# Attention of a decoder block: where the products with the values stand in the next group, and the order of the refills

## What is computed

```python
q = (x @ Wqa @ Wqb).reshape(b, s, H, D)
kv = (x @ Wkva @ Wkvb).reshape(b, s, KVH, D, 2)
k, v = (kv[..., 0], kv[..., 1])
q = _rope(q); k = _rope(k)
scores = jnp.einsum('bqhd,bkhd->bhqk', q, k) * scale     # causal mask
w = jax.nn.softmax(scores, axis=-1)
out = jnp.einsum('bhqk,bkhd->bqhd', w, v).reshape(b, s, E)
```

## Time and profile before

| | us |
|---|---|
| median of three runs | 1338.8 |
| the profiled execution, device time | 1340.68 |
| its span | 1338.7 |
| PE, DVE, ACT, POOL busy | 1062.5, 798.1, 660.4, 423.2 |
| attention: first Exp to the last copy of sums | 194.8 to 513.8 |

### The profile page before, as it was taken

One profiled execution on the slowest core, in us unless ns is written; L12 is line 12 of the kernel. 1 busy time (PEld: TensorE's weight loads), 2 busy tenths in 40 slices (PEclk: granted clock), 3 DMA queues, 4 the chain that ended last, 5 costly groups with the idle time before them and its releaser, 6 DMA issues. The chain is left out here.

```text
span 1338.7 us, 23286 instructions
## 1 busy us (share of the span) xinstructions
PE 1062.5 (79%) x7133; PEld 781.2 (58%) x7133; DVE 798.1 (60%) x1705; ACT 660.4 (49%) x1166; POOL 423.2 (32%) x556
## 2 busy tenths in 40 slices
PE   3777058788999984884478899898989989899886
PEld 2444023343444442773367788777878777788775
DVE  4888356576777762763446646656565565654643
ACT  1334115565666674562137355473654637447443
POOL 0344226566333331110344232332313333132301
PEclk9677558899999996897689899898999989999997
DMA  2332423333222204166411121101211012010000
GB/s 86 106 114 75 126 88 113 113 105 113 94 91 88 74 34 136 64 247 245 135 47 64 48 79 47 60 18 47 78 47 63 16 47 78 0 63 17 1 17 16
DMA packets 52989, 103.82 MB, mean 78 GB/s; under 512 B 6656, under 2 KB 32768, under 8 KB 48832
## 3 DMA queue, kind: packets, MB, share of 16 engines
q1 hardware_dynamic: 49756, 95.62, 21.0%
q0 software_dynamic: 1920, 6.03, 1.4%
q10 hardware_dynamic: 1252, 1.39, 0.3%
HBM read 63.05 MB, written 39.58 MB: 77 GB/s over the span
## 5 line engine op out<-in xcount | busy, mean ns | idle before, releaser
L802 ACT ACTIVATE p_probs<-p_psS 128x512 f32<-128x512 f32 (+1 forms) x352 | 181.2, 564 | 125.5 <-ACTq L801 122.9
L704 DVE CUSTOM_DVE_ANT_0 p_psA<-p_psA,p_mask 128x512 f32<-128x512 f32 (+1 forms) x256 | 155.7, 647 | 106.4 <-DVEq L702 106.0
L836 PE MATMUL p_psA<-p_ks,p_qs 96*128 96x512 bf16 (+3 forms) x512 | 145.1, 319 | 36.8 <-PEq L834 36.5
L855 PE MATMUL p_psS<-p_qs,p_ks 99*128 99x256 bf16 (+3 forms) x512 | 132.3, 312 | 21.7 <-PEq L880 12.5
L1658 ACT ACTIVATE p_h<-p_psG,w_columns 128x512 f32<-128x512 f32 x128 | 88.2, 689 | 121.6 <-ACTq L1657 121.0
L1995 PE MATMUL p_psY<-p_n,p_hh 128*128 128x256 f32 x512 | 117.2, 313 | 35.8 <-PEq L1986 29.7
L1773 DVE TENSOR_TENSOR p_hl<-p_h,p_hh 128x512 fp32r<-128x512 f32 x128 | 86.7, 687 | 88.9 <-DVEq L1772 86.6
L723 POOL TENSOR_SCALAR_AFFINE_SELECT p_probs<-p_probs 128x512 f32<-128x512 f32 x128 | 80.6, 634 | 134.1 <-POOLq L722 114.7
L1995 PEld LDWEIGHTS p_psY<-p_n,p_hh 128*128 128x128 f32 x512 | 95.6, 218 | 41.8 <-issue 41.3
L866 PE MATMUL p_psO<-p_probs,p_v 128*32 128x512 f32 (+3 forms) x1024 | 93.1, 458 | 26.4 <-PEq L862 25.1
L1571 POOL TENSOR_TENSOR p_var<-p_mv,p_eps 128x4 f32<-128x4 f32 x24 | 8.1, 338 | 334.0 <-POOLq L1577 201.8
(11 more groups left out here) (251 smaller groups left out, 2824.2 us busy)
## 6 DMA issues: line engine op xcount, KB each, us to landing
p_n<-n_parts SPq DMA_DIRECT2D x16, 1024.0 KB, 6.7
o_sums<-p_o SPq DMA_DIRECT2D x32, 256.0 KB, 2.7
n_parts<-p_nh SPq DMA_DIRECT2D x8, 1024.0 KB, 3.9
n_parts<-p_nl SPq DMA_DIRECT2D x8, 1024.0 KB, 6.0
q_parts<-p_part SPq DMA_DIRECT2D x48, 128.0 KB
p_qs<-q_parts SPq DMA_DIRECT2D x32, 192.0 KB
p_x<-in_x_dram SPq DMA_DIRECT2D x8, 512.0 KB, 4.4
p_qs<-q_parts SPq DMA_DIRECT2D x32, 128.0 KB
```

What stands on the lines that cost most here:

```text
L704: nc.vector.tensor_tensor_reduce(out=bank[:, 0:w], in0=bank[:, 0:w], in1=mask[:, S - w:S], scale=1.0, scalar=MASKED, op0=ALU.add, op1=ALU.max,
L802: nc.scalar.activation(probs[:, g % 2, at:at + n * w], psS[place(s, turn) % SB][:, 0:n * w], ACT.Exp, scale=SCALE).then_inc(exp_done, 1)
L836: last = nc.tensor.matmul(bank[:, z * w:(z + 1) * w], qs[0:SROWS, k, g * G + r0 + z, i * P:(i + 1) * P], ks[0:SROWS, k, g, 0:w], start=Tru ...
L855: last = nc.tensor.matmul(bank[:, z * w:(z + 1) * w], key, qs[0:SROWS + MROWS, k, h, j * P:S], start=True, stop=True)
```

## The change

Nothing is added to or taken from what is computed. Three things move:

- Values: in group n tiles 0 and 1 of group n-1 come at s = 1, tiles 2 and 3 at s = 5. None is left in group n for group n itself; after the last group all four tiles follow.
- The copy of the sums out of psO moves from after unit 4 to after unit 7.
- SP: after the maxima it loads queries and keys at once, then waits for the sums and stores them, then loads the values.

```diff
-        OUT_AT = 4
-        PV2_AT = 2
-        PV0_AT, PV1_AT = 7, 10
+        PV_AT = {1: (0, 1), 5: (2, 3)}
+        OUT_AT = 7
...
+        def load_values(queue, b, k, z):
+            two = slice(z * KVH // 2, (z + 1) * KVH // 2)
             queue.dma_start(v[:, k, two].rearrange("p g t n -> p (g t n)"),
...
-            def refill(b, k, g):
-                load_queries(b, k, g)
-                if g % 2 == 1:
-                    load_keys(sp, b, k, g // 2)
+            def turn_over(done, o_group, fresh):
+                if fresh is not None:
+                    b, k, g = fresh
+                    load_queries(b, k, g)
+                    if g % 2 == 1:
+                        load_keys(sp, b, k, g // 2)
+                store(done, o_group)
+                if fresh is not None and g % 2 == 1:
+                    load_values(sp, b, k, g // 2)
...
-                        if s == PV2_AT and (g >= 1 or not first):
-                            for j in (2, 3):
-                                exps(start - RING + place(LAST[j]) + 1)
+                        if s in PV_AT and (g >= 1 or not first):
+                            for j in PV_AT[s]:
+                                if j == 0:
+                                    exps(start - RING + place(OUT_AT + 1) + 1)
                                 values(k if g >= 1 else 1 - k, (g - 1) % KVH, j)
-                        if s == PV0_AT:
-                            exps(start + place(OUT_AT + 1, turn) + 1)
-                            values(k, g, 0)
-                        if s == PV1_AT:
-                            exps(start + place(LAST[1], turn) + 1)
-                            values(k, g, 1)
...
-            for j in (2, 3):
+            for j in range(TT):
                 values(1, KVH - 1, j)
```

More of the change, by code:

```diff
@@ L660, in batch @@
                     if g >= 1:
-                        store(b, g - 1)
-                        if more:
-                            refill(b + 2, k, g - 1)
+                        turn_over(b, g - 1, (b + 2, k, g - 1) if more else None)
                     elif not first:
-                        store(b - 1, KVH - 1)
-                        if has_next:
-                            refill(b + 1, 1 - k, KVH - 1)
+                        turn_over(b - 1, KVH - 1, (b + 1, 1 - k, KVH - 1) if has_next else None)
                     if first and g + 1 < KVH:
@@ L774, in _ @@
                     load_keys(act, k, k, z)
+                    load_values(act, k, k, z)
             for i in range(2):
@@ L869, in values @@
                     last.then_inc(O_ready, 1)
-            WAITED = (KVH - 1) * RING + place(LAST[1]) + 1
+            WAITED = KVH * RING - SB
             def batch(k, first, has_next):
```

## The result

The kernel after takes 1353.7 us (median of four runs, 1352.53 to 1358.35), the kernel before beside it 1339.45 (1336.12 to 1343.97). The ratio is 1.0117, with a 95% interval of 1.0092 to 1.0141: slower by 14 us, about 1%, and clear of the noise. The forecast was 1342, its range ended at 1352. The profiled execution took 1354.66 us, its span is 1352.7. That is 14.0 us more than the span before.

What follows compares the result with a forecast made beforehand. PE was taken to have the least slack in attention, with the maxima's DMA behind the line deciding. +2.1 + 5.2 - 0.8 - 1.5 - 3.1 + 0.8 = +2.7 us on the profiled 1340.7; given as 1342, range 1326 to 1352.

Steps and rivals of the forecast that it cites:

- The products alone: Attention groups with nothing else in the way: about 8.5 us each in place of 9.11, worth 0.6 us per group.
- The line: Groups 12 to 25: queries, keys and values delay the maxima's DMA; pairs take 18.7 us against 18.4, +2.1 us (-1 to +6).
- The clock: Pairs with refills: PE stands 2.35 us, the clock may fall; four falls in eleven pairs at 1.3 us, +5.2 (0 to +18).
- The early groups: Groups 0 to 3: line starts sooner, -0.8 us; groups 4 to 11: POOL's round keeps nearly all waits, -1.5 us.
- Groups 26 to 31 and the tail: Groups without refills gain, -3.1 us (-4.5 to -1); four tiles left after the last group cost +0.8 us (0 to 1.5).
- Rival 1: Same line, but the clock falls in nearly every pair: eleven falls, +9 to +12 us more, 1351 to 1354; chance 0.15.

Runs made afterwards that it cites:

- filled gaps: Kernel after, but PE repeats the last unit of row scores four times more in every second group (1.9 us of matmuls): 1341.35 us, 1.0018 of before.
- few-bytes: Kernel after, but each refill of queries loads only the first 128 queries of its group's first head, with as many DMAs: 1306.48 us, 0.977 of before.
- six-DMA: Kernel after, but stacked query copies loaded by six DMAs of 16 partitions instead of three, keys issued ahead of them: 1292.06 us, a second time 1291.85.
- later products: Kernel after, but tiles 0 and 1 at s = 4, tiles 2 and 3 at s = 7, copy of the sums after unit 9: 1361.28 us, 1.016 of before.

## Why the prediction was too low

**The products alone: right.** A free group was to take 8.5 us, with the maxima 4.80 after its start and the next group 3.6 later. Where no line and no fall is in the way, the kernel after has 8.5 to 8.7, 4.82 (416.43 to 421.25) and 3.68; without the line the change gains half a microsecond a group, where 0.6 was worked out.

**The line: right.** 13.9 us from the first maxima of a pair to the second group's start was the forecast, 13.94 is the case shown (392.30 to 406.24). PE's wait was to be 2.35 us and is 1.93 to 2.18 in the pairs that go at full length. With a held clock 18.7 us a pair was forecast, 18.5 to 19.2. The one pair whose clock held took 18.43, a tenth under it, and the pairs with filled gaps take 18.9 to 19.1; so with a held clock the change would have brought nothing in groups 12 to 25, as said, or lost a little. The reason I gave for why the change could not reach its 8.5 us while the refills stood is what the few-bytes and six-DMA kernels show.

**The clock: wrong in number.** This is the step that failed. I took four falls in eleven pairs at 1.3 us, +5.2. There were ten. From 263 to 468 us stretches at half clock, 3.4 us long (one of 6.8), begin 20.4 to 20.5 us apart, with one left out near 345 us. The two rows I had were a stall of 1.5 us without a fall and one of 2.2 with it; I put 2.35 "at the upper one" and yet gave the rival in which it always falls 0.15. That had no reason in the profile. The price of one fall was nearly right: it is some 1.5 us where I had 1.3. The start of the second group to the next maxima is 6.4 to 6.6 us, and 5.0 where the clock held, in the one pair of this kernel (346.57 to 351.55) and in the kernel with filled gaps, because the long run, 1.0 us more, and ACT, which it leaves standing for 2.64 us in group 20, both lie on the path. The other half microsecond between the pair of 18.43 and those of 20.4 is the line: 13.45 us in that pair (333.12 to 346.57), 13.8 to 14.2 in the others. Why it was shorter once stays open.

ACT's Exp behind the long run in that group:

```profile
411.07 1.08 ACT L810 ACTIVATE p_probs<-p_psS 128x512 f32<-128x512 f32 x2 [2.64 <-ACTq L809]
```

Groups 12 to 25 lost 12.9 us. Six of their seven pairs had a fall, at 1.5 us an estimate of 9 us; the rest, some 4, is the line and the free part of the pair, where +2.1 was forecast.

**The early groups: the size was a bit low, the reason wrong.** -0.8 and -1.5 were forecast, -2.6 (0.9 of it ahead of the first group) and -1.1 came. But I held that POOL's round of masks and weights bounds groups 4 to 11. With few bytes or six DMAs these groups took 8.5 to 8.7 us, but for group 6 with 9.1 or 9.2. POOL's waits in the kernel after and in the six-DMA kernel (what it waited for, us, times, longest; groups 0 to 11) show how the two hang together:

```profile
POOL w_w_hi L2251 <- DMA p_stage<-in_L_xattn_w_dram: 5.5, 3, 2.0
```

```profile
POOL w_w_hi L2251 <- DMA p_stage<-in_L_xattn_w_dram: 1.0, 1, 1.0
```

The pieces of the weights landed late with the line and nearly all in time without it; over all weights POOL's waits for them in these groups fell from 10.1 us to 1.0. So what I read as POOL being late was mostly the line again: rows 10 showed POOL waiting for a DMA, and I did not ask why that DMA was late.

**Groups 26 to 31 and the tail: wrong.** -3.1 (my terms give -3.0) and +0.8 were forecast. Groups 26 to 29 gained 0.4, since group 26 still started behind a wait and a fall (467.86 to 477.96, 10.1 us), and the rest lost 4.6. There the clock fell twice: the first fall makes a run 1.3 us longer, and the last run came behind a wait of 2.42 us at half clock, 4.01 in place of 2.29, another 1.7. Leaving four tiles to the end also makes the wait for the last Exp one long standing of PE. From the start of group 30 to ACT's last copy it is 18.1 us before, 22.9 in the kernel after, and 20.9 in the second run of the six-DMA kernel (445.52 to 466.38), whose last products went at full clock. So some 2.0 us hang on the last fall and 2.8 do not. How much of these 2.8 the first fall makes was not tried.

**The sum.** Of the 14.0 us between the spans, the forecast had 2.7; 11.3 are missing. Groups 12 to 25 account for some 5.6 of them (+12.9 where the line and all four falls were to make +7.3), everything from group 26 to the end of the attention for 6.5 (+4.2 for -2.3), and the stretch behind the attention for 0.5; the first stretch came out 1.4 better. By the prices above the clock is most of both large parts: six falls at 1.5 us where I had four at 1.3 make 3.8 of the 5.6, and the falls at group 26 and in the tail some 4.5 of the 6.5 (estimates from these rows). The kernel with filled gaps, without falls in the steady part, takes 1341.4 us. That this is nearly the 1342 of the forecast is chance, since it has 1.9 us of useless matmuls in every pair. Rival 1 is what happened, at 1351 to 1354 and by the mechanism described there; but its sum had nothing of the 6.5 us at the end, and three of the ten falls lie in early groups, which gained all the same. That it met the time is in part luck.

**The order of the issues** did no harm. With the old products the new order is worth some 2 us (ratio 0.9982), with the new ones about 35.

## What to carry to other kernels

Before work of the critical engine is moved, follow what the move delays on the way out: here the small DMA of the maxima, about 1 us later in its group, behind a line of transfers that a few engines carry. A transfer in stacked or broadcast form should be cut so that all engines carry it; that alone gave more than the reordering, and made the reordering pay. And price a new standing of PE as the wait and the slower work behind it: where the trace has an example of a fall after a shorter wait, a fall in every turn is at least as likely as one now and then; here it came in ten turns of eleven.

## What the runs showed of the hardware

- Falls of the clock can come once in every turn of a loop. In the kernel after, the six waits of 1.93 to 2.18 us were followed by half clock for 3.4 us every time, once in each pair, 20.4 us apart; one of 1.62 us (at 346.57) was not, nor one of 1.5 before the change. A fall makes the pair longer but not the line shorter, so the next pair has the same wait.
- The length of one wait did not decide alone: in the kernel with filled gaps a wait of 2.06 us (at 284.70) was followed by full clock, and in the six-DMA kernel with the keys last one of 1.37 us (at 238.00) by half clock. With later products the clock fell at 431.9 us with no wait above 0.81 us ahead of it in that group.
- Longer waits went with longer falls: in the kernel with the new products and the old order the waits of 4.3 to 5.3 us at the starts of groups 8 to 24 each came with 6.8 us at half clock, the one of 6.5 us at group 12 with 10.2.
- A fall of 3.4 us cost about 1.5 us: 6.5 us from a start to the next maxima for 5.0, and groups of 11.1 to 11.3 us for 9.65 with later products.
- More work can be less time: 1.9 us of matmuls for nothing in each pair's wait took 12 us off.
- A transfer issued on POOL's queue was late because of those on SP's: POOL's waits for pieces of that weight fell from 5.5 to 1.0 us in groups 0 to 11 when SP's transfers were spread.
- SP's issue of a plain DMA of 16 partitions took 0.45 us, of a stacked one of 16 to 48 partitions 0.72 on average.
